# A cross-attention layer with its input load two batches ahead, its value products in other slots, and half of the low parts on GpSimd

## The reference, cut to what matters

```python
def _L0_xattn_ref(x, latents, ...):        # called with x=ctx_1024, latents=layernorm(x)
    xn = _layernorm(x, gamma_media, beta_media)
    ln = _layernorm(latents, gamma_lat, beta_lat)
    q = ln @ Wq + bq
    k, v = split(concatenate([xn, ln], axis=1) @ Wkv + bkv)     # 8 heads of 128
    sim = einsum('bhid,bhjd->bhij', q * DH ** -0.5, k)
    out = einsum('bhij,bhjd->bhid', softmax(sim), v)
    return out @ Wo + bo
x = x + _L0_xattn_ref(...)
x = x + _L0_ffn_ref(_layernorm(x), ...)    # a feed-forward step with weights made from 16 rows
x = x + _L1_xattn_ref(...)                 # one more attention
x = x + _L1_ffn_ref(...)                   # 8 gated experts
```

## Time and profile before

| | |
|---|---|
| median of 3 runs | 2016.79 us (2014.29 to 2018.83) |
| the profiled execution | 2014.87 us, its span 2012.6 us |
| granted clock of TensorE, mean | 0.97 |
| TensorE matmul busy | 1843.4 us (92%) |
| VectorE busy | 1509.3 us (75%) |
| ScalarE busy | 1327.7 us (66%) |
| GpSimd busy | 396.6 us (20%) |

### The profile page before, as it was taken

One profiled execution on the slowest core, in us unless ns is written; L12 is line 12 of the kernel. 1 busy time (PEld: TensorE's weight loads), 2 busy tenths in 40 slices (PEclk: granted clock), 3 DMA queues, 4 the chain that ended last, 5 costly groups with the idle time before them and its releaser, 6 DMA issues.

```text
span 2012.6 us, 39933 instructions
## 1 busy us (share of the span) xinstructions
PE 1843.4 (92%) x12874; PEld 1694.2 (84%) x12874; DVE 1509.3 (75%) x3620; ACT 1327.7 (66%) x2554; POOL 396.6 (20%) x610
## 2 busy tenths in 40 slices
PE   6888888888888888989887999999999999999999
PEld 5777777776777777877776899999999999999998
DVE  6877776677677767766765778888888888888876
ACT  4766765676666667666755677777776676777753
POOL 1222222222122222221224511111111111111100
PEclk8999999999989999999998999999999999999999
DMA  4354534444444333333344394333333333333300
GB/s 139 67 128 91 128 97 102 113 110 116 99 120 104 79 79 79 67 83 77 80 86 103 90 295 82 72 70 75 75 81 81 80 70 65 80 80 81 81 7 12
DMA packets 355419, 182.24 MB, mean 91 GB/s; under 512 B 292512, under 2 KB 340512, under 8 KB 355360
## 3 DMA queue, kind: packets, MB, share of 16 engines
q1 hardware_dynamic: 346656, 146.88, 30.2%
q0 software_dynamic: 8704, 34.61, 9.6%
HBM read 97.29 MB, written 21.23 MB: 59 GB/s over the span
## 4 chain that ended last, share of the span: by engine, by line
PE 65%; DVE 14%; issue 8%; ACT 4%; DMA 3%; SPq 2%; POOL 1%; DVEq 0%; ACTq 0%; POOLq 0%
PE ring L2014 8%; PE ring L2016 8%; PE ring L2015 8%; PE ring L724 5%; PE ring L725 5%; PE ring L726 5%; DVE a_parts L645 4%; PE sim L2016 3%; PE sim L2014 3%; PE sim L2015 3%; DVE a_nmax L625 2%; DMA a_c_in<-in_ctx_in 2%; PE sim L724 2%; SPq L323 2%; PE sim L725 2%
## 5 line engine op out<-in xcount | busy, mean ns | idle before, releaser
L484 ACT ACTIVATE a_pr<-sim,a_nmax 128x512 f32<-128x512 f32 x256 | 173.9, 684 | 208.8 <-DVE a_nmax L625 208.1
L2014 PE MATMUL ring<-b_xch,b_wel 128*128 128x256 f32 x1024 | 289.9, 283 | 0.5 <-DVE b_act_e L1637 0.5
L2016 PE MATMUL ring<-b_xcl,b_weh 128*128 128x256 f32 x1024 | 286.5, 280 | 0.0
L2015 PE MATMUL ring<-b_xch,b_weh 128*128 128x256 f32 x1024 | 286.3, 280 | 0.0
L392 POOL TENSOR_SCALAR a_parts<-a_pr,a_rinv 128x512 f16<-128x512 f32 x240 | 170.6, 725 | 446.2 <-DVE a_rinv L636 431.8
L724 PE MATMUL sim<-a_kth,a_qth 128*128 128x512 f32 x256 | 116.9, 457 | 133.5 <-DVE a_qtl L607 112.1
L645 DVE SCALAR_TENSOR_TENSOR a_parts<-a_pr,a_rinv,a_parts 128x512 f16<-128x512 f32 x240 | 200.4, 875 | 19.8 <-POOL a_parts L392 18.5
L2015 PEld LDWEIGHTS ring<-b_xch,b_weh 128*128 128x128 f32 x1024 | 193.4, 189 | 0.0
L724 PEld LDWEIGHTS sim<-a_kth,a_qth 128*128 128x128 f32 x256 | 51.5, 201 | 167.9 <-issue 133.5
L2014 PEld LDWEIGHTS ring<-b_xch,b_wel 128*128 128x128 f32 x1024 | 192.2, 188 | 0.7 <-DVE b_act_e L1637 0.7
L2016 PEld LDWEIGHTS ring<-b_xcl,b_weh 128*128 128x128 f32 x1024 | 192.1, 188 | 0.0
(11 more groups left out here) (362 smaller groups left out, 6413.9 us busy)
## 6 DMA issues: line engine op xcount, KB each, us to landing
b_w2l_raw<-in_W2T POOLq DMA_DIRECT2D x16, 1088.0 KB, 8.6
b_even_b<-rows_between SPq DMA_DIRECT2D x16, 1024.0 KB, 5.5
b_w1l_raw<-in_W1T POOLq DMA_DIRECT2D x16, 1024.0 KB, 8.3
b_w1l_raw<-in_We SPq DMA_DIRECT2D x8, 768.0 KB, 6.0
expert_halves<-b_w1h SPq DMA_DIRECT2D x8, 768.0 KB, 3.5
expert_halves<-b_w1l SPq DMA_DIRECT2D x8, 768.0 KB, 4.7
b_weh<-expert_halves SPq DMA_DIRECT2D x8, 768.0 KB, 8.6
b_wel<-expert_halves SPq DMA_DIRECT2D x8, 768.0 KB, 10.0
```

The lines of the kernel that those rows point to most:

```text
L484: nc.scalar.activation(pr[:, h % 2, t, :], sim[t][:], ACT.Exp, bias=nmax[:, h % 2, t:t + 1], accum_out=rsum[:, h % 2, t:t + 1]).then_inc(e ...
L2014: nc.tensor.matmul(out, ll, rh, start=(n == 0), stop=False)
L2015: nc.tensor.matmul(out, lh, rh, start=False, stop=False)
L2016: last = nc.tensor.matmul(out, lh, rl, start=False, stop=(n == len(parts) - 1))
```

## The change

It has three parts. The loads of `c_in` and `x_in` for batch b + 2 are issued in turn b, after the transposes of head 5 (slot 4), and those for batch 1 ahead of the first transposes. V4 stays in slot 0, slot 1 has no V, V5 is in slot 2, V6 and V7 in slot 3; V0 to V3 stay in slots 6 and 7. The low part of the first 128 rows of a head stays on VectorE; that of the second 128 rows is made by GpSimd, which scales the exponentials in place, copies them with rounding into the high part, and subtracts the two. A new semaphore `pool_part` counts the in-place scaling and the subtraction. A semaphore `consts` is merged into `pool_step` (constants only).

```diff
@@ slot
-        if h < KT:
-            out.append(("V", KT + h))
-        if h >= H - 2:
-            out += [("V", 2 * (h - H + 2)), ("V", 2 * (h - H + 2) + 1)]
-        return out
+        return out + [("V", v) for v in {0: (4,), 2: (5,), 3: (6, 7), H - 2: (0, 1), H - 1: (2, 3)}.get(h, ())]
@@ sync: cross
-            for part, made, done in ((0, prob_ready, turned_hi), (1, part_lo, turned_lo)):
-                take(made, n * ST + ST)
+            for part, done in ((0, turned_hi), (1, turned_lo)):
+                if part == 0:
+                    take(prob_ready, n * ST + ST)
+                else:
+                    take(part_lo, n + 1)
+                    take(pool_part, n * 2 + 2)
@@ sync
+        def inputs_in(b):
+            take(ln_ready, b * 3)
+            sp.dma_start(c_in[:], c_t[b]).then_inc(in_c, 16)
+            sp.dma_start(x_in[:], x_t[b]).then_inc(in_x, 16)
+        inputs_in(1)
         cross(0, 0)
         def turn(order, b, prev, nxt, spare=False):
-            if nxt:
-                sp.wait_ge(ln_ready, b * 3 + 3)
-                sp.dma_start(c_in[:], c_t[b + 1]).then_inc(in_c, 16)
-                sp.dma_start(x_in[:], x_t[b + 1]).then_inc(in_x, 16)
-            else:
+            if not nxt:
                 other.beside(0, "begin")
...
                     cross(*head_after(b, h))
+                if h == 4 and nxt and not is_ahead(b):
+                    inputs_in(b + 2)
@@ gpsimd: normalise_probs
             for t in range(ST):
-                if crosses(b):
+                if crosses(b) and t == 0:
                     nc.gpsimd.tensor_scalar(parts[:, 0, t, :], pr[:, h % 2, t, :], rinv[:, h % 2, t:t + 1], 1.0,
                                             ALU.mult, ALU.mult).then_inc(prob_ready, 1)
+                elif crosses(b):
+                    nc.gpsimd.tensor_scalar(pr[:, h % 2, t, :], pr[:, h % 2, t, :], rinv[:, h % 2, t:t + 1], 1.0,
+                                            ALU.mult, ALU.mult).then_inc(pool_part, 1)
+                    take(pool_part, n * 2 + 1)
+                    nc.gpsimd.tensor_copy(parts[:, 0, t, :], pr[:, h % 2, t, :]).then_inc(prob_ready, 1)
+                    if not (isinstance(b, int) and b == 0 and h == 0):
+                        take(turned_lo, n * 16)
+                    take(prob_ready, n * ST + ST)
+                    nc.gpsimd.tensor_tensor(parts[:, 1, t, :], pr[:, h % 2, t, :], parts[:, 0, t, :],
+                                            ALU.subtract).then_inc(pool_part, 1)
@@ scalar: exps
+                if t == 1 and not (isinstance(b, int) and (b == 0 and h < 2 or b == B - 1 and h > 1)):
+                    act.wait_ge(pool_part, (b * H + h) * 2 - 2)
@@ vector: inverses
                 dve.wait_ge(prob_ready, n * ST - ST)
+                if not (isinstance(b, int) and b == B - 1 and h > 1):
+                    dve.wait_ge(pool_part, n * 2 - 2)
@@ vector: low_parts
-            for t in range(ST):
-                dve.wait_ge(prob_ready, n * ST + t + 1)
-                nc.vector.scalar_tensor_tensor(parts[:, 1, t, :], pr[:, h % 2, t, :], rinv[:, h % 2, t:t + 1],
-                                               parts[:, 0, t, :], ALU.mult, ALU.subtract).then_inc(part_lo, 1)
+            dve.wait_ge(prob_ready, n * ST + 1)
+            nc.vector.scalar_tensor_tensor(parts[:, 1, 0, :], pr[:, h % 2, 0, :], rinv[:, h % 2, 0:1],
+                                           parts[:, 0, 0, :], ALU.mult, ALU.subtract).then_inc(part_lo, 1)
```

More of the change, by code:

```diff
@@ L234, in latent_attention @@
     affine_in, c_small, bo_in = sem("affine_in"), sem("c_small"), sem("bo_in")
-    consts = sem("consts")
     w_hi, w_lo, bq_ready = sem("w_hi"), sem("w_lo"), sem("bq_ready")
@@ L244, in latent_attention @@
         sem(n) for n in ("sim_full", "max_ready", "exp_done", "inv_ready", "prob_ready"))
+    pool_part = sem("pool_part")
     part_lo, turned_hi, turned_lo, cast = sem("part_lo"), sem("turned_hi"), sem("turned_lo"), sem("cast")
@@ L374, in gpsimd @@
         nc.gpsimd.affine_select(out=ident[:], in_=ident[:], compare_op=ALU.not_equal, fill=1.0, base=0,
-                                pattern=[[-1, P]], channel_multiplier=1).then_inc(consts, 1)
+                                pattern=[[-1, P]], channel_multiplier=1).then_inc(pool_step, 1)
         def rstd_of(b, k):
@@ L381, in rstd_of @@
                 .then_inc(pool_step, 1)
-            pool.wait_ge(pool_step, b * 3 + k + 3)
+            pool.wait_ge(pool_step, b * 3 + k + 4)
             nc.gpsimd.tensor_tensor(rstd[:, k, :], veps[:, k, :], mhalf[:], ALU.pow).then_inc(rstd_ready, 1)
@@ L802, in project_out @@
                 last.then_inc(wo_full, 1)
-        pe.wait_ge(consts, 1)
+        pe.wait_ge(pool_step, 3)
         transposes(0)
@@ L854, in fill_count @@
         return last.at(at + last.names[at:].index(name)) + 1
-    names = ("consts", "kv_ready", "x1_ready", "x1_out", "ring_full", "ring_lo", "sim_full", "exp_done", "wo_full", "took")
-    sems = dict(zip(names, (consts, kv_ready, x1_ready, x1_out, ring_full, ring_lo, sim_full, exp_done, wo_full, took)))
+    names = ("kv_ready", "x1_ready", "x1_out", "ring_full", "ring_lo", "sim_full", "exp_done", "wo_full", "took")
+    sems = dict(zip(names, (kv_ready, x1_ready, x1_out, ring_full, ring_lo, sim_full, exp_done, wo_full, took)))
     return FirstHalf(sync, gpsimd, scalar, vector, tensor, ident, mhalf, (ring, sim, ps_c, ps_x), sems, fill_count)
```

## The result

| | before | after |
|---|---|---|
| median, 4 runs of each | 2016.86 us (2014.29 to 2018.83) | 1899.64 us (1898.54 to 1900.94) |
| ratio, 95% interval | | 0.942 (0.9403 to 0.9436) |
| span profiled, mean granted clock | 2012.6 us, 0.970 | 1898.0 us, 0.988 |

1899 was forecast. Windows of the kernel after, the same stretches as the earlier trace rows: start:end, length, then busy time (instructions) of PE, PEld, DVE, ACT and POOL, then clock, DMA share and GB/s.

What follows compares the result with a forecast made beforehand. Waits in the sixteen turns, for the load and VectorE's chain, plus TensorE's low clock were the bound. Gains of 66 + 42 + 5 + 5 sum to 118 us, giving 1899 us; own range 1880 to 1915.

Steps and rivals of the forecast that it cites:

- The load: Slots 0 and 1: loading two turns ahead ends VectorE's wait, gaining 3.5 us, and slot 1's slow stretch, gaining 1.8.
- the chain I named: Slots with a Q: start of the maxima to the next scores takes 4.75 us, the next thing to be late.
- The value products: Slots 1 to 3: moving V5 and V6 loses the 0.5 us wait and 0.2 more in slot 2.
- The low parts: GpSimd takes one low part per head in 4.0 us; slot 4 becomes 8.3 us with an expert, 7.1 without.
- no slow stretch behind it: Slot 4's idle of 1.6 or 0.4 us leaves the clock up, so slot 5 becomes 5.2 us.
- rival C: GpSimd becomes the bound: two slots take at least L + 8.4 us; L = 9.0 reaches today's 8.7 per slot; chance 0.05.
- The port: GpSimd instructions can block VectorE's remaining low part for their length; it takes 0.75 us in V-fill slots, 1.15 in slot 4.
- The tight place: Slot 5: the low part lands 6.8 us after the slot's start, fitting by 0.1 to 0.3 us.
- Turn 14: Gains 5.5 us in slots 0 to 4 and keeps its 14.5 us stall; 5 in all.
- A: GpSimd's added instructions block VectorE for their whole length, no low-part relief in any slot: 1933 us; chance 0.20.
- B: All TensorE idle time in the turns goes, 57.6 us a turn: 1858 us; chance 0.08.
- D: Expert's weights or the x1 store hold SyncE, so slot 0 stays: 1976 us; chance 0.05.

Runs made afterwards that it cites:

- the smaller dose: Kernel after the change with two more small GpSimd instructions per head ahead of the subtraction, their output unused: 1917.0 us, ratio 0.9533.

## Why the prediction was right, and where its steps were not

The mechanism held: the wait for the load ended slot 0, it pulled the clock down in slot 1, and VectorE's list set the ends of slots 2 to 5. The sum had 118 us; the spans of the two profiles differ by 114.6 and the medians by 117.2, so that 1899 was met to within 1 us is in part luck.

- **The load.** I had 3.5 + 1.8 us per turn; by itself it gives 75 us in all, 4.9 in each of turns 1 to 8, where slot 5 took 0.55 us back at the lower clock, and 5.6 in each of turns 9 to 13. Behind it came the chain I named: 347.46 - 342.70 = 4.76 us from the maxima to the next scores. With the low part relieved the maxima start 2.21 us after the slot's start, not 2.65, and TensorE's own pace ends the slot.
- **The value products.** This step failed in size and in sign, hidden inside a right sum. I had "Net: slots 1 to 3 lose the 0.5 us wait and 0.2 more in slot 2", a small gain, beside the 1.4 us of slot 1 that come back in slot 3. The runs show 15 to 17 us of gain where VectorE makes both low parts and 8 us of loss in this change. Both come from what VectorE's instructions meet on GpSimd at the start of slot 4. What I did not follow was GpSimd's sequence from slot 3 into slot 4: I had VectorE's low part ended at 2.3 us and the third at 3.5 after the slot's start; measured 2.27 and 3.84, since the third took 1.65 us beside the subtraction, and I had 1.2.
- **The low parts.** Slot 4 forecast 8.3 and 7.1, measured 8.52 and 7.52. Its idle was 1.94 us where I had 1.6, and so "no slow stretch behind it" held in only half of turns 1 to 8: four of them have a slot 5 of 6.3 to 6.7 us. Without an expert the idle time was 0.95 us where I had 0.4. GpSimd's sequence of 3.8 us (346.87 to 350.67 in turn 5) lay in my 3.5 to 4.0; it is four instructions a head, and the "five" of the prediction, in the port's paragraph and in rival C, is a miscount that the sum didn't use. The port: over the rows below, the single low part has a median of 0.93 us, not the 0.743 of the earlier trace rows.

```profile
L662 DVE SCALAR_TENSOR_TENSOR a_parts<-a_pr,a_rinv,a_parts x120: 740/930/1620, 28.6 to 958.8; 128x512 f16<-128x512 f32 x120
L402 POOL CAST a_parts<-a_pr x120: 607/614/1142, 29.5 to 958.6; 128x512 f16<-128x512 f32 x120
L406 POOL TENSOR_TENSOR a_parts<-a_pr,a_parts x120: 1151/1175/2187, 30.5 to 959.4; 128x512 f16<-128x512 f32 x120
```

  Of the 70 low parts and thirds that begin during a GpSimd copy or subtraction in the kernel after, 66 end 0.54 or 0.55 us behind it. By the Trainium skill (SBUF — State Buffer, Who interferes with whom) a VectorE instruction with two SBUF inputs is shut out while a GpSimd instruction that reads SBUF holds the shared port. The 66 of 70 agree with it.
- **The tight place** of slot 5 was as forecast: ScalarE's low cast waits for the landing nine times in 100 to 1000 us, 3.7 us in all. But idle time was to be left at the end of slots 2 and 4 only, and TensorE also has 0.7 to 0.8 us of it at the end of slot 5, in every turn from 2 to 13 (1.2 in turn 9).
- **Turn 14** gained 3.1 us, not 5. I had counted SyncE's issues there but not that a shorter slot 1 brings VectorE to its next wait earlier. The rows' load is issued at 902.66; VectorE came to the statistics 2.94 us before they could run, slot 2 got 3.80 us of idle and slot 3 the low clock (9.35 us):

```profile
902.66 0.43 SPq L1085 DMA_DIRECT2D b_first_rows<-x_between  x1
...
905.21 0.42 DVE L1611 BATCH_NORM_STATS2 b_row_stats<-b_first_rows 32x6 f32<-32x256 f32 x1 [2.94 <-DMA b_first_rows<-x_between]
...
910.72 0.76 PE L741 MATMUL sim<-a_kth,a_qth 128*128 128x512 f32 x1 [3.80 <-DVE a_qtl L623]
```

- **Rivals.** A is refuted by the low parts' 32 and 49 us. B (1858) names what no version reached; the chain of 4.76 us still ends slots 2 and 4. C is real as a mechanism: five small instructions more per head on GpSimd (3.7 us) cost 114 us. But today's 8.7 us per slot is reached earlier than at my "L = 9.0", with sequences of 7.2 and 7.9 us (660.82 to 668.03, 643.44 to 651.34), by the circle through the transpose. D is refuted by the load alone.

Open: turn 1 after is 1.3 us longer than turn 2 (its slot 0 takes 8.8 us) and turn 0 kept 2 to 3 us of idle in each of three slots; no experiment was made for either. The parts without the load but with the products were not run, so the table has one empty field. Why the smaller dose spreads over 19 us from run to run wasn't followed up.

## What to carry to other kernels

When an edit shifts work into another slot, follow the list of the engine it relieves or fills past the slot's end, and note which instruction of the other SBUF engine it then falls beside: here GpSimd's addition coming 0.6 to 1.3 us earlier in slot 4 was half of a gain of 17 us, and a third that met GpSimd's subtraction instead of its copy, with the slow stretches behind it, was a loss of 8. Parts of one change should be priced in each other's presence; here the load made the low parts worth 49 us instead of 32, and a right total hid a wrong sign. After a wait is removed, ask of every later instruction what fixed event it now reaches too early.

## What the runs showed of the hardware that was not expected

- A VectorE instruction of 128 by 512 with two SBUF inputs that started during a GpSimd copy, addition or subtraction of that size ended 0.54 to 0.55 us after it in nearly all cases: a third took 1.09 us beside a copy and 1.65 beside a subtraction, in place of 0.68.
- It goes the other way too. In the kernel after, the 51 GpSimd copies that began while such a VectorE instruction ran took 0.83 us or more, the other 69 0.61; of the subtractions 44 took 1.38 us or more, the others 1.17 (median).
- The third was not held up by a GpSimd instruction of 128 by 2: with two of them ahead of the subtraction, seven thirds of one kernel began during one, took their usual 0.68 us, and the GpSimd instruction took 0.92 in place of 0.69.
- The idle time of TensorE alone does not tell whether the lower clock follows. Behind 1.92 to 1.98 us it did in four turns and not in four others with the same instructions. Behind 2.6 us ahead of slot 5 it did in three of turns 1 to 8 of the kernel before and in all eight with the load moved. 1.6 us or less was followed by none in turns 1 to 13 of the kernel without the products' move. In turns 1 to 13 of the kernels that had it 3.7 us and more was followed by one every time but one: behind 3.70 us in turn 9 of the kernel with the products alone, slot 1 took 9.74 us at full clock.
- GpSimd's added float16 copy took 0.61 us and the wait on its own semaphore between two dependent instructions 0.17 to 0.19 us.
